# Attention stage: TensorE's side jobs cut into halves and given new slots, keys projected one batch ahead, rope steps placed between masks

## What is computed

```
def attention(x, w_qkv, w_out):            # x: layer norm of the stage's input, B=8, S=512, D=128
    q, k, v = split(x @ w_qkv)             # 16 heads of 8
    q, k = rope(q), rope(k)                # x1*cos - x2*sin, x2*cos + x1*sin
    scores = where(causal, q @ k.T * 8**-0.5, lowest)
    attn = softmax(scores)
    return (attn @ v) @ w_out
```

## Time and profile before

| what | us |
|---|---|
| median of 3 runs (976.91 to 978.07) | 977.78 |
| profiled execution | 977.11 |
| its span | 975.4 |
| TensorE busy, of the span | 764.3 |
| VectorE busy | 633.9 |
| ScalarE busy | 523.8 |
| GpSimd busy | 419.5 |

### The profile page before, as it was taken

How to read it: one execution, slowest core, us unless ns; L and a number is a source line. 1 busy time by engine, 2 the same in 40 slices (tenths; PEclk the granted TensorE clock), 3 DMA queues, 4 the chain that set the end, 5 groups by cost and what they waited for, 6 DMA issues and landing times.

```text
span 975.4 us, 18027 instructions
## 1 busy us (share of the span) xinstructions
PE 764.3 (78%) x5550; PEld 507.5 (52%) x5550; DVE 633.9 (65%) x2291; ACT 523.8 (54%) x1435; POOL 419.5 (43%) x537
## 2 busy tenths in 40 slices
PE   3789992987699902997929788888988999729977
PEld 3679991646599901775813233333333433317757
DVE  4555546685744469554797577777877885585534
ACT  4435542424255418665201576866767777687650
POOL 2046751301467524110376658668576533261100
PEclk9999995995699965999965699989989999859999
DMA  6741113002111130000044324122242200000002
GB/s 158 218 109 48 52 42 91 1 22 65 30 49 52 42 92 1 1 1 1 8 59 55 45 35 62 29 46 44 30 63 32 38 3 4 1 1 1 1 2 87
DMA packets 52526, 41.99 MB, mean 43 GB/s; under 512 B 9224, under 2 KB 48080, under 8 KB 52432
## 3 DMA queue, kind: packets, MB, share of 16 engines
q1 hardware_dynamic: 46784, 31.74, 16.4%
q0 software_dynamic: 4096, 8.40, 2.9%
q10 hardware_dynamic: 1552, 0.70, 0.3%
HBM read 17.35 MB, written 10.49 MB: 29 GB/s over the span
## 4 chain that ended last, share of the span: by engine, by line
PE 54%; DVE 15%; ACT 9%; POOL 7%; issue 7%; DMA 3%; SPq 2%; ACTq 1%; DVEq 0%; POOLq 0%
PE psum L814 8%; PE psum L827 7%; PE psum L1525 5%; PE psum L1296 3%; PE psum L1259 3%; PE psum L768 3%; PE psum L1268 3%; DVE cst L1592 3%; PE psum L1510 2%; DVE half_stats L447 2%; DVE x L717 2%; PE psum L1359 2%; PE psum L1465 2%; PE psum L1497 2%; ACT arena L1654 2%
## 5 line engine op out<-in xcount | busy, mean ns | idle before, releaser
L1592 DVE CUSTOM_DVE_ANT_0 cst<-psum,rot 128x512 bf16<-128x512 f32 (+3 forms) x512 | 219.3, 487 | 67.0 <-PE psum L1497 58.1
L1654 ACT ACTIVATE arena<-psum 128x512 f32<-128x512 f32 (+1 forms) x384 | 178.4, 530 | 54.2 <-PE psum L1510 48.7
L1497 PE MATMUL psum<-arena 48*128 48x512 bf16 (+3 forms) x512 | 121.3, 329 | 17.7 <-DVE row_max L1592 10.9
L1510 PE MATMUL psum<-arena 51*128 51x512 bf16 (+3 forms) x512 | 114.4, 314 | 11.5 <-ACT arena L1654 6.9
L740 ACT ACTIVATE arena<-psum,gate_b1T 128x128 f32<-128x128 f32 x234 | 68.8, 365 | 74.7 <-PE psum L814 74.7
L853 POOL DMA_INDIRECT arena<-xhat_rows,token_of x64 | 61.8, 966 | 104.5 <-DVE token_of L658 81.0
L1749 POOL TENSOR_SCALAR_AFFINE_SELECT arena<-arena 128x384 f32<-128x384 f32 x128 | 63.6, 521 | 96.1 <-ACT arena L1654 96.1
L1525 PE MATMUL psum<-arena 128*32 128x512 f32 (+3 forms) x1024 | 98.3, 482 | 6.7 <-POOL arena L1752 6.7
L814 PE MATMUL psum<-arena 128*128 x624 | 87.8, 286 | 4.9 <-issue 2.8
L827 PE MATMUL psum<-arena 128*128 x624 | 86.7, 282 | 0.5 <-ACT arena L740 0.5
L814 PEld LDWEIGHTS psum<-arena 128*128 128x128 f32 x624 | 78.9, 199 | 9.8 <-issue 9.6
(11 more groups left out here) (249 smaller groups left out, 1636.9 us busy)
## 6 DMA issues: line engine op xcount, KB each, us to landing
arena<-cut SPq DMA_DIRECT2D x192, 64.0 KB
xhat_rows<-xh SPq DMA_DIRECT2D x16, 256.0 KB, 2.3
arena<-result_rows SPq DMA_DIRECT2D x8, 512.0 KB, 6.0
x<-in_L_attn_x SPq DMA_DIRECT2D x4, 512.0 KB, 7.7
arena<-in_L_ffn_w SPq DMA_DIRECT2D x1, 2048.0 KB, 9.5
out<-x SPq DMA_DIRECT2D x4, 512.0 KB, 3.2
arena<-xhat_rows,token_of POOLq DMA_INDIRECT x64, 2.5
result_rows<-arena,token_of POOLq DMA_INDIRECT x64
```

The source lines that it names most:

```text
L1497: mm = pe.matmul(to[:, col:col + (k + 1) * P], q_stack[b % STACKS][rows, h, k * P:k * P + P], k_stack[b % STACKS][rows, h, 0:(k + 1) * P], ...
L1510: mm = pe.matmul(bank[MAX_BANKS + number % EXP_BANKS][:, col:col + S - k * P], k_stack[b % STACKS][rows, h, k * P:k * P + P], q_stack[b % ...
L1592: last = nc.vector.tensor_tensor_reduce(masked_scores[:, number % 2, col:col + n_keys], frm[:, col:col + n_keys], mask[:, S - n_keys:], 1. ...
L1654: nc.scalar.activation(prob_e[g % 2][:, j, first:last], bank[MAX_BANKS + number % EXP_BANKS][:, 0:last - first], ACT.Exp, scale=DH ** -0.5 ...
```

## The change

`JOBS` gets entries of (slot, turn, step, batch, range of 128-column tiles, last piece?). The four matmuls `p` and `s` of batches from 2 on become two of 256 columns each, `v` of batches from 1 on and `wo` become two pieces of two tiles; only the last piece raises `misc_mm`, only the first waits for the bank. The readers stay whole and stand in the slot of the last piece. In a body `i` of the middle of the stage the slots now are: 0 `v` of batch `i` (turns 0 and 2), 1 `m1`, 2 and 3 `p1` of batch `i + 1` (turns 2 and 0), 4 `s1` (turns 0 and 2), 5 `n0`, 6 `n1`, 7 `to`, 8 `wo` (turns 1 and 2), 9 `m0`, 10 `xt` of batch `i + 2`, 11 and 12 `p0` (turns 2 and 0), 13 and 14 `s0` (turns 0 and 2). So queries are projected two bodies ahead as before, keys one. On GpSimd both ropes of batch `i + 1` now lie in body `i`, two steps before each mask from pair 2 to pair 7, and SP's transfers follow that order.

```diff
+            def halves(i, first, second, step, b):
+                JOBS[i].append((*first, step, b, (0, TB // 2), False))
+                JOBS[i].append((*second, step, b, (TB // 2, TB), True))
+            def single(i, at, step, b):
+                JOBS[i].append((*at, step, b, (0, TB), True))
...
             for b in range(B):
-                    at_body, at_slot = (b - 2,) * 5, (10, 11, 12, 13, 14)
-                JOBS[b] += [(7, "v", b), (9, "m0", b)]
+                if b:
+                    halves(b, (0, 0), (0, 2), "v", b)
...
+                if b >= 2:
+                    single(b - 2, (10, 2), "xt", b)
+                    halves(b - 2, (11, 2), (12, 0), "p0", b)
...
                 def job(step, b, m, tiles=(0, TB), ends=True):
                     to = bank[misc_bank(m)]
+                    cols = slice(P * tiles[0], P * tiles[1])
+                    if tiles[0]:
+                        pass
-                    if 1 <= m < 5:
+                    elif 1 <= m < 5:
...
-                        last = pe.matmul(to[:], w[:, int(step[1]), :], xT[:, b % 2, :], start=True, stop=True)
+                        last = pe.matmul(to[:, cols], w[:, int(step[1]), :], xT[:, b % 2, cols], start=True, stop=True)
...
-                    last.then_inc(s["misc_mm"], 1)
+                    if ends:
+                        last.then_inc(s["misc_mm"], 1)
...
                 for i in range(B + 1):
-                    keys_next = 1 if i >= 1 and i + 1 < B else 0
+                    ahead = 1 <= i < B - 1
                     if i:
                         cut_maxima(i - 1, 1)
                         causal(i - 1, 1)
+                    for part in range(3):
+                        if ahead:
+                            rotate(pool, pool, i + 1, 0, 2 * part, 2 * part + 2)
+                        if i:
+                            causal(i - 1, 2 + part)
+                    for part in range(3):
+                        if ahead:
+                            rotate(pool, pool, i + 1, 1, 2 * part, 2 * part + 2)
+                        if part == 1 and i < B:
+                            cut_maxima(i, 0)
+                        if i:
+                            causal(i - 1, 5 + part)
                     if i < B:
                         causal(i, 0)
-                    if i + 2 < B:
-                        rotate(pool, pool, i + 2, 0, 3, 6)
...
                 for i in BODIES[1:]:
                     if 1 <= i <= B:
                         maximum(i - 1, 1)
+                    if 1 <= i < B - 1:
                         for part in range(3):
+                            stack_part(sp, i + 1, 0, part)
+                        for part in range(2):
                             stack_part(sp, i + 1, 1, part)
                     if 0 <= i < B:
                         maximum(i, 0)
+                    if 1 <= i < B - 1:
+                        stack_part(sp, i + 1, 1, 2)
```

More of the change, by code:

```diff
@@ L1385, in attention, with whole @@
             JOBS = {i: [] for i in BODIES}
-            for b in range(B):
-                steps_in = ("xt", "p1", "s1", "p0", "s0") if b == 0 else ("xt", "p0", "s0", "p1", "s1")
-                if b < 2:
-                    at_body, at_slot = ((-1,) * 5, (0, 1, 2, 3, 4)) if b == 0 else ((-1, 0, 0, 0, 0), (5, 0, 1, 2, 3))
-                else:
-                    at_body, at_slot = (b - 2,) * 5, (10, 11, 12, 13, 14)
-                for step, i, slot in zip(steps_in, at_body, at_slot):
-                    JOBS[i].append((slot, step, b))
-                JOBS[b] += [(7, "v", b), (9, "m0", b)]
-                JOBS[b + 1].append((1, "m1", b))
-                JOBS[b + 2] += [(2, "n0", b), (4, "n1", b), (6, "to", b), (8, "wo", b)]
+            def whole(i, slot, step, b):
+                JOBS[i].append((slot, 1 if slot % 2 == 0 else 2, step, b, (0, TB), True))
+            def halves(i, first, second, step, b):
[3 more added lines that the diff above has]
+                JOBS[i].append((*at, step, b, (0, TB), True))
+            for slot, step in enumerate(("xt", "p1", "s1", "p0", "s0")):
+                whole(-1, slot, step, 0)
+            whole(-1, 5, "xt", 1)
+            for slot, step in enumerate(("p0", "s0", "p1", "s1")):
+                whole(0, slot, step, 1)
+            whole(0, 7, "v", 0)
+            for b in range(B):
+                if b:
+                    halves(b, (0, 0), (0, 2), "v", b)
+                single(b, (9, 2), "m0", b)
+                single(b + 1, (1, 2), "m1", b)
+                single(b + 2, (5, 1), "n0", b)
+                single(b + 2, (6, 2), "n1", b)
+                single(b + 2, (7, 2), "to", b)
+                halves(b + 2, (8, 1), (8, 2), "wo", b)
+                if b >= 2:
+                    single(b - 2, (10, 2), "xt", b)
+                    halves(b - 2, (11, 2), (12, 0), "p0", b)
+                    halves(b - 2, (13, 0), (14, 2), "s0", b)
+                    halves(b - 1, (2, 2), (3, 0), "p1", b)
+                    halves(b - 1, (4, 0), (4, 2), "s1", b)
             for i in BODIES:
@@ L1400, in attention, with pieces_at @@
             for i in BODIES:
-                for slot, step, b in JOBS[i]:
-                    ORDER[step, b] = len(ORDER)
+                for slot, turn, step, b, tiles, last in JOBS[i]:
+                    if last:
+                        ORDER[step, b] = len(ORDER)
             def jobs_at(i, hh):
-                return [(step, b, ORDER[step, b]) for slot, step, b in JOBS[i] if slot == hh]
+                return [(step, b, ORDER[step, b]) for slot, turn, step, b, tiles, last in JOBS[i] if slot == hh and last]
+            def pieces_at(i, hh, turn):
+                return [(step, b, ORDER[step, b], tiles, last) for slot, at, step, b, tiles, last in JOBS[i] if (slot, at) == (hh, turn)]
             def maxing(i):
@@ L1449, in tensor, with job @@
             def tensor(pe, only_first=False):
-                def job(step, b, m):
+                def job(step, b, m, tiles=(0, TB), ends=True):
                     to = bank[misc_bank(m)]
-                    if 1 <= m < 5:
+                    cols = slice(P * tiles[0], P * tiles[1])
+                    if tiles[0]:
+                        pass
+                    elif 1 <= m < 5:
                         pe.wait_ge(s["misc_read"], 1)
@@ L1459, in job @@
                     if step == "xt":
-                        for k in range(TB):
+                        for k in range(*tiles):
                             pe.wait_ge(s["normed"], TB * b + k + 1)
@@ L1476, in job @@
                         pe.wait_ge(s["sums_read"], 2 * (b + 1))
-                        for i in range(TB):
+                        for i in range(*tiles):
                             k = 2 * int(step[1]) + i // 2
@@ L1534, in side @@
                         sums(*found, SUM_AT[hh % 4, turn])
-                    if turn == (1 if hh % 2 == 0 else 2):
-                        for step, b, m in jobs_at(i, hh):
-                            job(step, b, m)
+                    for step, b, m, tiles, ends in pieces_at(i, hh, turn):
+                        job(step, b, m, tiles, ends)
                 if only_first:
@@ L1856, in sync @@
                         maximum(i - 1, 1)
-                    if i >= 1 and i + 1 < B:
+                    if 1 <= i < B - 1:
                         for part in range(3):
+                            stack_part(sp, i + 1, 0, part)
+                        for part in range(2):
                             stack_part(sp, i + 1, 1, part)
@@ L1861, in sync @@
                         maximum(i, 0)
-                    if i + 2 < B:
-                        for part in range(3):
-                            stack_part(sp, i + 2, 0, part)
+                    if 1 <= i < B - 1:
+                        stack_part(sp, i + 1, 1, 2)
             first_batch[n] = dict(tensor=lambda pe: tensor(pe, True), vector=lambda dve: vector(dve, True))
```

25 lines of the change are left out of this document (3 added, 22 removed).

## The result

| what | before, us | changed, us |
|---|---|---|
| median (lowest to highest) of 20 runs each | 977.35 (975.53 to 982.96) | 984.47 (974.88 to 1005.96) |
| ratio of the change to before, 95% interval | | 1.0047 (1.0025 to 1.0068) |
| profiled execution, its span | 977.11, 975.4 | 995.26, 993.5 |

The change is slower, by about half a per cent; the forecast was 959 us. The interval leaves the most disturbed runs out, which matters here, since the changed kernel scatters over 31 us where the kernel before scatters over 7. Rival 3 in full, the first maxima late, gave 980 us.

What follows compares the result with a forecast made beforehand. No engine is full; VectorE waits 9 to 10 us a body for TensorE, in slots 1 and 2 and 9 to 14. Terms -12.3 - 10.3 + 2.6 + 1.8 = -18.2 from 977.1 gave 959 us, range 949 to 972.

Steps and rivals of the forecast that it cites:

- Rival 3: Slot 12, bodies 1 to 6: first maxima arrive late, TensorE stalls 3.8 us each; 980 us, slower than before; chance 0.06.
- Term a: Body borders, slots 1 and 2: TensorE's clock stays at 1.00 with slots 14 and 0 filled; -12.3 us over bodies 1 to 6.
- Rival 1: Body borders: the clock still falls, TensorE being paced there by VectorE's banks; 971 us; chance 0.15.
- Term d: First maxima behind two rope steps and ten key transfers: 0.3 us stall a body, six times; +1.8 us.
- Term b: Slots 9 to 14, bodies 0 to 5: halved projections cut 1.7 of 3.30 us of TensorE's excess; -10.3 us.
- the sign for the right case: Slots 9 to 14 taking 13.5 us, listed among the observations that would show the forecast right.
- The half's price of 0.63: Half a projection on TensorE taken at 0.63 us, between half of 1.06 and 1.06; not in the trace.
- Rival 2: Slots 2, 3, 11 and 13: halves cost 1.06 us each, like wholes; +10 us, 969 us; chance 0.06.
- The waits for the jobs' shared bank are hidden: First halves come a turn or more after the previous job's reader; VectorE's filled banks cover 1.65 us; no cost counted.
- A head's maxima and exponentials cost 0.65 us: TensorE's price per head, read as 619.01 - 618.36, used in the sums for slots 9 to 14.
- Slot 12 fits, and the cut is just in time: Slot 12 needs 1.28 us of TensorE against VectorE's 1.645; two rope steps leave the maxima's cut 0.1 us in hand.
- Term c: Slots 0 to 8, bodies 1 to 6: moved jobs add 0.44 us a body; +2.6 us, bounds 0 and +6.

Runs made afterwards that it cites:

- Experiment 6: The kernel before, with only the value projection moved, in two halves, from slot 7 to slot 0; 960.87 us, ratio 0.9849.
- experiment 2: The changed kernel with SP's order alone edited: first maxima's transfer ahead of the four transfers of the keys' part 1; 969.23 us, ratio 0.9928.
- experiment 7: The kernel of experiment 2 with the first halves of `s0` and `s1` one turn later; 962.39 us, ratio 0.9859.
- experiment 8: The kernel of experiment 2 with GpSimd's cut of the first maxima ahead of the keys' rope steps 2 and 3; 966.77 us, ratio 0.9905.

## Why the prediction was wrong, point by point

**Term a, the clock at the borders (-12.3): right.** The clock stands at 1.00 there, slots 1 and 2 took 4.85 us where about 5 were named. Experiment 6 has it by itself, with 12.1 us. Rival 1 is out: with work in slot 0 the clock did not fall.

**Term d, GpSimd and the first maxima (+1.8): the step that failed.** Measured between the change and experiment 2 it is 13 us. The prediction took 3.5 us from issue to use and a stall of 0.3 a body. Two things were wrong with it.
- The size of the stall. I argued that six of the ten transfers were some slots old. They were 7.6 us old (651.71 against 659.28), but the last four end where the maxima's begin. That follows from the new order itself: the cut stands right behind the rope step that releases part 1, so the two always meet. From issue to use 4.75 us were needed in body 3; the stalls were 0.62 to 2.51 us in bodies 1 to 6, between my 0.3 and rival 3's 3.8.
- What a stall costs. I priced one at its own length, in the rival too. Slots 11 to 14 lost 4.9 us for 1.88 of waiting, as the clock fell behind it. In body 2, where the wait was 0.62, slot 13 took 2.89 us, as without a stall.

How much of the 4.75 us is bandwidth shared with the key transfers, and how much the order in which completions are signalled, which the prediction named as the mechanism, no run separates.

Rival 3 was the right mechanism at the right place, and its 980 us lies close to the 982 to 984 measured, but by compensation: shorter stalls, dearer each, and gains below 20.0. The scatter fits the same cause, since a slightly longer wait decides on several microseconds of low clock; I did not take profiles of enough runs to show that for it.

**Term b, slots 9 to 14 (-10.3): the second step that failed.** Without stalls (experiment 2, body 3) these slots take 14.23 us, less one product of 0.94 is 13.29; before it was 15.23 - 1.88 = 13.35. The gain is 0.06 us a body, not 1.7. (The 13.5 us that I named as the sign for the right case was itself a slip: it still held both products, and with the keys' moved to slot 4 it should have read 12.6.) The half's price of 0.63 was right. TensorE in the change, a half and the first half of `s1`:

```profile
640.42 0.70 PE L1494 MATMUL psum<-xT,wqk 128*128 128x256 f32 x2
641.05 0.33 PE L1540 MATMUL psum<-arena 51*128 51x384 bf16 x1
...
643.44 0.70 PE L1494 MATMUL psum<-xT,wqk_turned 128*128 128x256 f32 x2 [0.78 <-ACTq L1697]
```

641.05 - 640.42 = 0.63. Rival 2 is out in its own terms. Three other things were wrong here.
- *The waits for the jobs' shared bank are hidden.* They are not: the last line has 0.78 us of TensorE waiting for ScalarE's read of the job before. 9.8 us of such waits lie between 560 and 800 (10.4 in experiment 2), where the kernel before has 0.9:

```profile
PE psum L1465 <- ACTq L1668: 0.9, 5, 0.2
```

A turn's delay (experiment 7) took the waits to 3.7 and gave back 6.8 us of time. I had written that without cover each would cost about half a microsecond; the cover was assumed from order, without asking when ScalarE, in its own queue, comes to the read. In slots 9 to 14 that is 0.23 us a body (slot 13), in slot 4 it is 0.55.
- *A head's maxima and exponentials cost 0.65 us.* Where a whole head stands beside sums or a job, the kernel before has 616.99 - 616.46 for three pieces and 620.02 - 619.80 for the fourth, 0.53 + 0.22 = 0.75:

```profile
616.46 0.39 PE L1510 MATMUL psum<-arena 51*128 51x512 bf16 x1
...
616.99 0.85 PE L1525 MATMUL psum<-arena 128*32 128x384 f32 x8
```

The 0.1 is missing in slots 9, 10, 11 and 13; slots 10 and 11 took 2.13 and 2.17 us where 2.02 and 2.07 were worked out.
- *Slot 12 fits, and the cut is just in time.* Slot 12 took 1.99 us where 1.645 were taken, and slot 9 a quarter of a microsecond more than with the cut first (experiment 8).

About 0.4 us in slot 13 and 0.17 in slot 14 stay unexplained.

**Term c, slots 0 to 8 (+2.6): right in sum, by errors that cancel.** Body 3 without the low clock took 23.29 - 2.65 = 20.64 us for these slots before, and 21.90 now, of which 0.94 is the product moved there: +0.32 a body against the +0.44 taken. In its parts it was not: slots 1 and 2 came out shorter than worked out, and slot 4, "under VectorE's own work", takes 3.65 us where 1.645 + 0.94 = 2.59 was its floor. About half of that excess, 0.55 us, is the bank wait again (experiment 7).

**The sum.** With what was measured, -12.1 - 0.4 + 1.9 + 13 = +2.4 us; the change measured +5. Some 2.5 us lie outside these terms, among them slot 0 of body 1, which takes 3.4 us where it took 1.65.

## What to carry to other kernels

Before small, urgent transfers are placed behind bulk ones, look at when the last bulk transfer is released, not at how many there are; here ordering them in the one queue cured it, and another issuing engine did not. Price a wait of TensorE with the clock it may cost, and look for the places where it runs ahead and idles: one job moved into such a gap gave more here than the whole redesign. Where several jobs share a buffer, take each reader's time from its own engine's queue before cutting jobs finer.
